# Attention output normalised transposed, one step later: reciprocal of the sums in slot 9, output and gamma rows on GpSimd's queue

## The reference

```python
def _sln(h, w, ln_g, ln_b, Wg, bg, Wb, bb):
    mu = jnp.mean(h, axis=-1, keepdims=True)
    var = jnp.mean((h - mu) ** 2, axis=-1, keepdims=True)
    ln = (h - mu) / jnp.sqrt(var + EPS) * ln_g + ln_b
    gamma = (w @ Wg.T + bg)[:, None, :]
    beta = (w @ Wb.T + bb)[:, None, :]
    return gamma * ln + beta
h = _sln(hidden, w, ln_g, ln_b, Wg, bg, Wb, bb)
qkv = (h @ Wqkv.T + bqkv).reshape(B, N, num_heads, hd, 3)
# q, k, v: the last axis, heads moved ahead of the tokens
energy = jnp.einsum('bhqd,bhkd->bhqk', q, k)
att = jax.nn.softmax(energy, axis=-1) / D ** 0.5
out = jnp.einsum('bhqk,bhkd->bhqd', att, v)
out = jnp.moveaxis(out, 1, 2).reshape(B, N, D)
out = out @ Wp.T + bp
h1 = out + hidden
h2 = _sln(h1, w, ln_g, ln_b, Wg, bg, Wb, bb)
return h2 + h1
```

## Time and profile before

| what | value |
|---|---|
| median of 3 runs | 347.56 us (345.03 to 347.65) |
| the profiled execution's own time | 345.56 us |
| its span | 343.8 us |
| PE busy | 332.5 us, 97% |
| PE's weight loads busy | 286.8 us, 83% |
| DVE busy | 298.3 us, 87% |
| ACT busy | 242.8 us, 71% |
| POOL busy | 159.1 us, 46% |
| DMA | 48.87 MB, 142 GB/s over the span |
| granted clock of PE | 1.0 of full speed |

### The profile page before, as it was taken

How to read it: one execution, slowest core, us unless ns; L and a number is a source line. 1 busy time by engine, 2 the same in 40 slices (tenths; PEclk the granted TensorE clock), 3 DMA queues, 4 the chain that set the end, 5 groups by cost and what they waited for, 6 DMA issues and landing times.

```text
span 343.8 us, 8981 instructions
## 1 busy us (share of the span) xinstructions
PE 332.5 (97%) x3173; PEld 286.8 (83%) x3173; DVE 298.3 (87%) x728; ACT 242.8 (71%) x476; POOL 159.1 (46%) x187
## 2 busy tenths in 40 slices
PE   8888999999999999999999999999999999999993
PEld 4677879888888988888888988888898988888773
DVE  4888978799898989899898989989898988999684
ACT  7664876868676786868686876868687786766740
POOL 5765544437164545527264644617254643224330
PEclk9999999999999999999999999999999999999999
DMA  7396445456555454555545454655556354652021
GB/s 242 126 218 186 124 115 140 129 155 157 170 141 156 134 152 135 173 156 170 142 125 169 134 155 134 184 142 160 161 135 157 98 157 123 182 146 67 16 61 61
DMA packets 47705, 48.87 MB, mean 142 GB/s; under 512 B 6287, under 2 KB 41374, under 8 KB 47662
## 3 DMA queue, kind: packets, MB, share of 16 engines
q1 hardware_dynamic: 44494, 46.74, 49.2%
q10 hardware_dynamic: 1184, 1.07, 1.2%
q0 software_dynamic: 1984, 0.51, 0.8%
HBM read 9.99 MB, written 4.23 MB: 41 GB/s over the span
## 4 chain that ended last, share of the span: by engine, by line
PE 87%; DVE 5%; DMA 3%; ACT 1%; issue 1%; ACTq 1%; SPq 0%; DVEq 0%
PE m L976 24%; PE st L976 19%; PE sa L976 18%; PE pv L976 17%; PE pv L1065 4%; DVE mx L692 3%; PE pv L1146 2%; PE m L1105 2%; DMA wqkv<-WqkvT_dram 2%; DMA kst<-qk_l 1%; PE pv L1079 1%; PE m L1079 1%; ACT p L602 0%; DVE qk_l L727 0%; ACTq L625 0%
## 5 line engine op out<-in xcount | busy, mean ns | idle before, releaser
L692 DVE TENSOR_REDUCE mx<-sa 128x2 f32<-128x512 f32 x256 | 171.5, 684 | 28.4 <-PE sa L976 27.3
L602 ACT ACTIVATE p<-st 128x512 f32<-128x512 f32 x240 | 140.9, 598 | 37.5 <-PE st L976 33.2
L976 PE MATMUL sa<-kst,qst 126*128 126x256 f32 x512 | 105.6, 288 | 2.0 <-DMA kst<-qk_l 1.0
L976 PE MATMUL st<-qst,kst 128*128 128x256 f32 x496 | 104.1, 292 | 0.2
L976 PEld LDWEIGHTS st<-qst,kst 128*128 128x128 f32 x496 | 75.1, 188 | 13.8 <-issue 12.8
L976 PEld LDWEIGHTS sa<-kst,qst 126*128 126x128 f32 x512 | 78.6, 189 | 4.6 <-DVE mx L692 1.7
L368 POOL DMA_DIRECT2D qst<-m_h x31 | 17.6, 567 | 112.4 <-DVE m_l L701 112.4
L976 PE MATMUL pv<-p,v_st 128*32 128x256 f32 x1008 | 61.0, 382 | 0.0
L976 PEld LDWEIGHTS pv<-p,v_st 128*32 128x32 f32 x1008 | 29.5, 109 | 21.0 <-ACT p L602 1.5
L976 PE MATMUL m<-hT_h,wqkv_h 128*128 128x256 f32 x128 | 36.8, 300 | 1.3 <-ACT hT_h L616 0.7
L377 POOL TENSOR_SCALAR xn<-xa,mv,rstd 128x256 f32<-128x256 f32 x28 | 34.2, 1227 | 1.5
(11 more groups left out here) (149 smaller groups left out, 566.2 us busy)
## 6 DMA issues: line engine op xcount, KB each, us to landing
qst<-qk_h SPq DMA_DIRECT2D x64, 128.0 KB, 2.4
qst<-qk_l SPq DMA_DIRECT2D x64, 128.0 KB, 2.5
kst<-qk_h SPq DMA_DIRECT2D x62, 128.0 KB, 2.5
kst<-qk_l SPq DMA_DIRECT2D x62, 128.0 KB, 2.8
xa<-x_dram SPq DMA_DIRECT2D x16, 256.0 KB, 3.0
gb<-gb_rows SPq DMA_DIRECT2D x16, 256.0 KB, 3.9
out_dram<-y SPq DMA_DIRECT2D x15, 256.0 KB, 3.4
wqkv<-WqkvT_dram SPq DMA_DIRECT2D x1, 512.0 KB, 5.6
```

The source lines that it names most:

```text
L602: nc.scalar.activation(p32[:, h, :], st_ps[h % 2][:], ACT.Exp).then_inc(exp_done, 1)
L692: dve.tensor_reduce(mx[:, par(a), h // HH, (h % HH) * TT:(h % HH + 1) * TT], sa_ps[h % 2][:].rearrange("p (t n) -> p t n", t=TT), AX.X, AL ...
L976: return nc.tensor.matmul(o, l, r, start=start, stop=stop)
```

## The change

For the items 0 to 13 (`by_transfer`) the output is no longer turned by token. The columns of `v_st` are interleaved (v, constant, v, constant), and `by_rows` reorders the rows of the projection's weights and the bias of v to match. SP moves the 64 channel rows of a group from `oT` into `o_rows` (the memory of `wqkv`, which is free by then) and one row of sums for each head into `sums`, 128 x 32 (`send_out`). DVE takes one reciprocal in slot 9, two transfers gather it into `recs` (the memory of `wb`), one spreads it over 128 partitions into `o_rec` (the memory of `wg`), and DVE multiplies once, 128x512, in slot 3 of the next step. ACT makes the high part from it in slot 4, POOL the low part. The projection and the residual stages of an item come one step later. `norm1` of item b + 4 moves to slots 11 to 13, with a power of its own on POOL in slot 15. The output and the rows of gamma and beta are issued by POOL, in slot 13 (`send_y`, `send_gb`). Group 0 is evicted in slot 14. The products of the projection run with the low part of `att` last. Items 14 and 15 are still turned by token (`normalise_tokens`). The last step projects items 13, 14 and 15.

```diff
-S_MT1, S_AT, S_MT0, S_XT = 1, 10, 9, 10
+S_MT1, S_AH, S_MT0, S_XT = 1, 4, 9, 10
...
-NX = 6
-S_O1, S_O0 = 3, 12
-S_OT1, S_OT0 = 6, 14
+NX = 7
+S_O1, S_O0 = 3, 14
+OUT_PRODUCTS = [(l, r, k, t) for l, r in ((0, 0), (0, 1), (1, 0)) for k in range(2) for t in range(2)]
...
-        att = sb("att", [P, TT, D])
+        sums = sb("sums", [P, H * N // P])
+        recs = wb[0:2 * HH].rearrange("p k n -> p (k n)")
+        o_rows = [wqkv[:, :, D:2 * D], wqkv[:, :, 2 * D:3 * D]]
+        o_rec, att = wg, wqkv[:, :, 0:D]
...
+        def by_transfer(a):
+
+            return 0 <= a < B - 2
...
+            def send_out(a, g):
+
+                if not by_transfer(a):
+                    return
+                half_rows = slice(g * P // 2, (g + 1) * P // 2)
+                sp.wait_ge(oT_ready, 2 * a + g + 1)
+                wait(sp, recs_in, 32 * a)
+                sp.dma_start(sums[half_rows, :], oT[1:P:32, g, :]).then_inc(sums_in[g], 16)
+                wait(sp, aTh_ready, a - 1)
+                wait(sp, aTl_ready, a - 1)
+                sp.dma_start(o_rows[par(a)][half_rows], oT[0:P:2, g, :].rearrange("p (c n) -> p c n", c=2)).then_inc(o_in[g], 16)
+
+            def gather_rec(a):
+
+                if not by_transfer(a):
+                    return
+                sp.wait_ge(rec_ready, a + 1)
+                for n in range(2):
+                    sp.dma_start(recs[n:2 * HH:2, :], sums[:]).then_inc(recs_in, 16)
+
+            def spread_rec(a):
+
+                if not by_transfer(a):
+                    return
+                sp.wait_ge(recs_in, 32 * (a + 1))
+                wait(sp, rows_ready, a)
+                sp.dma_start(o_rec[:], recs.rearrange("r (d n) -> r d n", d=1)
+                             .broadcast_to([2 * HH, HD // 2, 2 * N])).then_inc(rec_in, 16)
...
+                    if g == 0 and t == 0:
+                        gather_rec(a - 3)
...
+                send_out(b - 1, 1)
                 if has(b + 4) and has(b):
                     wait(sp, xn_ready, 1 * (b + 2) + 1)
-                    wait(sp, h1_ready, 1 * (b - 2) + 1)
+                    wait(sp, h1_ready, 1 * (b - 3) + 1)
                     sp.dma_start(xbuf(b + 4), x_t[b + 4]).then_inc(x_in[(b + 4) % 4], 16)
...
+                if not has(b + 2):
+                    gather_rec(b - 1)
+                spread_rec(b - 1)
...
-                if has(b - 1):
-                    wait(sp, y_ready, 1 * (b - 3) + 1)
-                    if first(b - 1):
-                        sp.wait_ge(gb_out, 16)
-                    sp.dma_start(gb[:, par(b - 1)], gb_dram[b - 1].rearrange("(a n) -> a n", a=1)
-                                 .broadcast_to([P, 2 * D])).then_inc(gb_in[par(b - 1)], 16)
-                if has(b - 2):
-                    wait(sp, y_ready, 1 * (b - 2) + 1)
-                    sp.dma_start(out_t[b - 2], y[:, par(b - 2)]).then_inc(y_out[par(b - 2)], 16)
+                send_out(b, 0)
...
+            def send_gb(a):
+
+                if first(a):
+                    pool.wait_ge(gb_out, 16)
+                wait(pool, y_ready, 1 * (a - 2) + 1)
+                pool.dma_start(gb[:, par(a)], gb_dram[a].rearrange("(a n) -> a n", a=1)
+                             .broadcast_to([P, 2 * D])).then_inc(gb_in[par(a)], 16)
+
+            def send_y(a):
+
+                wait(pool, y_ready, 1 * a + 1)
+                pool.dma_start(out_t[a], y[:, par(a)]).then_inc(y_out[par(a)], 16)
...
+            def low_att(a):
+
+                wait(pool, aTh_ready, a + 1)
+                pool.tensor_tensor(aT_l[:], o_rows[par(a)], aT_h[:], ALU.subtract).then_inc(aTl_ready, 1)
...
+                    if h == 0 and has(b - 1):
+                        add_bias(b - 1)
+                    if h == 1 and has(b) and has(b + 3):
+                        norm_x(b + 3)
+                    if h == 4 and by_transfer(b - 2):
+                        low_att(b - 2)
+                    if h == 5 and has(b - 3):
+                        rstd_out(b - 3)
...
-                    if h == 6 and has(b - 2):
-                        add_beta(b - 2)
-                    if h == 5 and has(b + 3) and has(b):
-                        norm_x(b + 3)
-                    if h == 0 and has(b - 1):
-                        add_bias(b - 1)
+                    if h == 6 and has(b - 3):
+                        add_beta(b - 3)
+                    if h == 15 and has(b + 4):
+                        rstd_x(b + 4)
                     if h in (13, 14) and b == B - 2:
                         add_bias(b + h - 13)
                     if h == 12:
                         low_h(b + 3)
+                    if h == 13 and has(b - 3):
+                        send_y(b - 3)
+                    if h == 13 and has(b - 2):
+                        send_gb(b - 2)
 
...
+                wait(act, o_in[g], 16 * a)
                 nc.scalar.activation(oT[:, g, :], pv_ps[g][:], ACT.Copy).then_inc(oT_ready, 1)
+
+            def high_att(a):
+
+                wait(act, rows_ready, 1 * a + 1)
+                wait(act, proj_done, 1 * (a - 1) + 1)
+                nc.scalar.activation(aT_h[:], o_rows[par(a)], ACT.Copy).then_inc(aTh_ready, 1)
...
-                    if h == S_AT + 1 and has(b - 1):
-                        wait(act, attT_done, 1 * (b - 1) + 1)
-                        wait(act, proj_done, 1 * (b - 2) + 1)
-                        nc.scalar.activation(aT_h[:].rearrange("p k n -> p (k n)"), pv_ps[1][:],
-                                             ACT.Copy).then_inc(aTh_ready, 1)
+                    if h == S_AH and has(b - 2):
+                        high_att(b - 2)
...
+            def reciprocal(a):
+
+                if not by_transfer(a):
+                    return
+                for g in range(2):
+                    wait(dve, sums_in[g], 16 * (a + 1))
+                dve.reciprocal(sums[:], sums[:]).then_inc(rec_ready, 1)
+
+            def normalise(a):
+
+                if not by_transfer(a):
+                    return
+                for g in range(2):
+                    wait(dve, o_in[g], 16 * (a + 1))
+                wait(dve, rec_in, 16 * (a + 1))
+                dve.tensor_tensor(o_rows[par(a)], o_rows[par(a)], o_rec[:], ALU.mult).then_inc(rows_ready, 1)
+
+            def normalise_tokens(a, g):
...
-                    (3, 0): [lambda: residual(b - 2, 0), lambda: residual(b - 2, 1)],
-                    (4, 0): [lambda: residual(b - 2, 2), lambda: norm1(b + 3, 0)],
-                    (4, 1): [lambda: residual(b - 2, 3), lambda: norm1(b + 3, 1)],
-                    (5, 0): [lambda: norm1(b + 3, 2)],
+                    (3, 0): [lambda: residual(b - 3, 0), lambda: residual(b - 3, 1), lambda: normalise(b - 2)],
+                    (4, 0): [lambda: residual(b - 3, 2)],
+                    (4, 1): [lambda: residual(b - 3, 3)],
                     (5, 1): [lambda: low_qk(b + 2, 0, m0, qh_ready, ql_ready)],
-                    (7, 0): [lambda: normalise(b - 1, 1, 0)],
+                    (9, 0): [lambda: reciprocal(b - 1)],
                     (7, 1): [lambda: low_qk(b + 2, 1, m1, kh_ready, kl_ready)],
-                    (8, 0): [lambda: normalise(b - 1, 1, 1)],
-                    (9, 1): [lambda: residual(b - 2, 4)],
-                    (11, 0): [lambda: low_max(b + 1, 0), lambda: low_att(b - 1), lambda: residual(b - 2, 5)],
-                    (15, 0): [lambda: normalise(b, 0, 0)],
-                    (15, 1): [lambda: normalise(b, 0, 1)],
+                    (9, 1): [lambda: residual(b - 3, 4)],
+                    (12, 1): [lambda: norm1(b + 4, 1)],
+                    (13, 1): [lambda: norm1(b + 4, 2)],
+                    (10, 1): [lambda: low_max(b + 1, 0), lambda: residual(b - 3, 5)],
+                    (11, 0): [lambda: norm1(b + 4, 0)],
                 }
+                if b == B - 2:
+                    between[(15, 0)] = [lambda: normalise_tokens(b, 0)]
                 if first(b):
                     between[(1, 1)] = between.pop((2, 1))
                 if first(b + 1):
...
+            residual(B - 4, 0)
+            low_max(B - 1, 1)
+            normalise(B - 3)
+            for stage in (1, 2, 3):
+                residual(B - 4, stage)
+            last_out(B - 2, 1)
+            residual(B - 4, 4)
+            normalise_tokens(B - 2, 1)
+            residual(B - 4, 5)
             residual(B - 3, 0)
-            low_max(B - 1, 1)
...
+            def project_out(a, quarter):
+
+                for n in range(3 * quarter, 3 * quarter + 3):
+                    l, r, k, t = OUT_PRODUCTS[n]
+                    if n == 0:
+                        wait(pe, aTh_ready, a + 1)
+                    if n == 8:
+                        wait(pe, aTl_ready, a + 1)
+                    o = mm(m1[:, t * D:(t + 1) * D], (aT_h, aT_l)[l][:, k, t * P:(t + 1) * P], (wp_h, wp_l)[r][:, k, :],
+                           n == 0, n == 11)
                 if quarter == 3:
...
```

(18 more changed lines are left out.)

160 lines of the change are left out of this document (78 added, 82 removed).

## The result

The changed kernel takes 350.78 us (median; 346.82 to 359.69), the kernel before 345.12 us (345.00 to 347.65), beside each other on one chip. The ratio is 1.0121 with a 95% interval of 1.0095 to 1.0147. The forecast of 330.5 us, range 326 to 342, was wrong by 20 us and in sign. The profiled execution took 350.8 us, its span is 348.9 (before 345.6 and 343.8). Medians are taken over all executions of a kernel, ratios and intervals only over those within 1.5% of its fastest one.

The account below looks back on a forecast made before the run. PE, busy for all 19.50 us of a middle step, was taken as the bound. 345.6 - 18.5 (transposes) + 1.3 (small waits) + 1.2 (last step) = 329.6 us; forecast as a median 330.5, range 326 to 342.

Parts of the forecast that it names:

- The price of the transposes: On PE, three groups of 0.44 us leave per item: 1.32 us a step, 18.5 us over 14 items.
- POOL's sends: Two added 128-row transfers issued by POOL in a step, expected at 0.5 to 1.1 us each, costing PE nothing.
- T: POOL's time for both sends in a step: 1 to 2 us taken, bounds 1.04 and 8.3, harmless under 2.2.
- The product on DVE: New 128x512 product in slot 3, priced at 0.748 us; a rival had `norm_x` holding it, 338 us, chance 0.08.
- Reserve 0.7 to 1.4 us: nothing is lost: SP's group 0 of the next stack, two gathers in between: data land before `scores_max` of head 0 needs them.
- SP's queue is late: Rival: slower landing or a gather's wait makes group 0 up to 0.7 us late, 13 steps, 339 us; chance 0.12.
- some 2 us of reserve: SP's group 1 of the stack starts about 1 us later, behind `send_out` of group 0, covered until slot 8.
- DMA engines are still a third idle: Argument against SP's queue is late: added bytes raise the DMA share only from 0.54 to 0.69.
- The last steps: Last step: added residual work on DVE and POOL costs 1.2 us, with bounds 0 to 4.7.
- Idle time is nearly twice the work: Last step: DVE's 8.8 us idle against 0 to 4.7 us added, the reason for taking 1.2 near the low end.

Follow-up runs that it names:

- kernel 3: The changed kernel with the spread of the reciprocals cut to 16 of 128 partitions (32 KB for 256, output wrong): nine of its 12 steps take 18.2 us.
- kernel 18: The kernel with the tiny transfers, its spread cut to 16 of 128 partitions (output wrong): 34.3 us less by the medians, 12 steps in 219.4 us.
- the kernel with the tiny transfers: Kernel 11 plus three four-byte transfers in SP's queue where gathers and spread stood: 376.93 us.
- 11: The changed kernel with the two gathers and the spread issued by ACT on its own queue, slots 10 and 13: 342.59 us, ratio 0.9873.
- 13: Kernel 11 with gamma rows and output issued by SP again, behind k: 338.57 us, ratio 0.9786.
- 15: The changed kernel with the spread alone issued by ACT (slot 14), the gathers staying on SP: 358.78 us.
- 16: The changed kernel with gamma rows and output issued by SP again, gathers and spread staying on SP: 354.33 us.
- 4: The kernel before with all transfers of the change added, results unused, POOL sending gamma rows and output: 350.79 us, ratio 1.0166.
- 10: The changed kernel with the last two sends (gamma rows of item 15, output of item 14) on SP: median hardly moved, executions 343.37 to 353.58 us.
- 5: The kernel before with output and gamma rows issued by POOL in slot 13 and not by SP, nothing else: 348.54 us.
- kernel 2: The changed kernel with gathers and spread issued by POOL (slots 10 and 13) in place of SP: 346.67 us.
- 17: The kernel with the tiny transfers, POOL's middle-item output and gamma rows cut to 8 of 128 partitions (output wrong): 14.6 us less by the medians.

## Why the prediction was wrong

**What held.** The price of the transposes: 18.2 us for a step, in nine steps of kernel 3, and 14.0 of 14.6 us in kernel 18. POOL's sends: 0.56 and 0.59 us each, T = 1.15, inside the 1 to 2 taken. The product on DVE: 675 ns for 748, and not held by `norm_x`. From the groups by shape of the changed kernel:

```profile
L789 DVE TENSOR_TENSOR wqkv<-wqkv,wg 128x512 f32<-128x512 f32 x14 | 9.5, 675 | 0.2 <-DMA wg<-wb 0.2
L441 POOL DMA_DIRECT2D gb<-gb_rows x16 | 9.0, 560 | 0.0
L447 POOL DMA_DIRECT2D out_dram<-y x15 | 8.9, 591 | 5.1 <-DVE y L905 5.1
```

**The step that failed is SP's** ("Reserve 0.7 to 1.4 us: nothing is lost"). It was made of medians and undisturbed pairs: issues of 0.6 to 0.68 us, a landing of 2.8. Its slot and its mechanism were named right, and the rival "SP's queue is late" had 0.12 with a price of 9 us. The stall above, beside the forecast: from SP's first transfer of group 0 the tenth should start after 5.4 to 6.1 us, land after up to 8.9 and be needed after 9.6; it started after 6.9 (247.02 to 253.94; the first pair alone took 2.23), landed after 11.1 and was needed after 8.9. The late start of the tenth is 0.8, the landing 1.4, the earlier need 0.7, less 0.7 of reserve: 2.2 us, the stall. The pair of 1.88 us in the kernel before stands in the very group that was priced at 5.5 us. Three numbers were wrong. The landing that counts is that of the transfer PE waits for, 4.16 in the stall above with a median of 2.7 on the page: in that stall the output, the gamma rows and the spread are in flight just then, because POOL sends in slot 13 what SP had sent behind k. The issue of the rows soon after the spread costs up to 2.5 us instead of 0.63; group 1, to which I gave "some 2 us of reserve", begins behind it, and waits of 0.5 to 1.4 us in slot 8 follow. And "DMA engines are still a third idle" weighed bytes: the spread was counted as 256 KB like any other, by the 3.9 us of the gamma rows. It lands after 4.6 us at best, and per byte it takes nearly three times the engines' time.

**What is shown of the cause:** cutting the spread's size gives back 5.7 of the 8.2 us missing in the 12 steps where it stands in SP's queue (3), and in the kernel with the tiny transfers all that they had cost (18); taking gathers and spread out of SP's queue gives back 4.9 and 5.4 with all bytes in place (11, 13), but the spread alone out of it makes things worse (15); more time for issues on SP makes PE wait though k lands fast (16); the same transfers under steps of 19.5 us cost the steps nothing (4). So both the queue and the spread's engine time take part, and they become visible only once PE's step is shorter. What draws an issue out is not shown: the kernel before and 3 and 18, with their small spreads, have pairs of 1.9 to 2.2 us too, at other places. A stall also costs more than its length: in kernel 3 two stalls of 2.2 and 2.8 us lengthened their steps by 3.9 and 3.6 (22.1 against 18.2, and 21.3 against 17.7 for the same step in 18), the clock being at its lower level for part of what follows (in the second PE waits for `mx` as well).

**The last steps** had 1.2 us, with bounds 0 to 4.7. Without the kst stalls (18) the last three steps cost 51.4 - 49.1 = 2.3, and the tail without its stall (10, 13) 16.0 - 14.4 = 1.6: 3.9 us, within the bounds and three times the value taken. "Idle time is nearly twice the work" was no reason: the work is a chain of small steps between DVE and POOL, and PE waits for its end. The changed kernel's own tail has another 2.8 for `xn` and the low clock, in the profiled execution; in eight variants it has not, and their end is 1.9 longer instead. Tail and end together lost 5.5 us in it and 4.9 to 5.0 in those.

**The end** was no term at all. In every kernel in which POOL sends the rows (5 has nothing else), apart from kernel 2, the execution ends some 2.5 us later after POOL's last instruction; in the changed kernel 1.1 of it shows as "end", since the slow last products on PE come after that instruction, and the rest is hidden in the tail.

In sum for the profiled executions: 12 steps -6.4 in place of -14.6, the rest up to the tail's end +0.5 + 5.6 + 4.4, the end +1.1.

## What to carry to other kernels

When the bounding engine's list gets shorter, the transfers behind it lose the same time: price the cover of each by the slowest landing in company with what will be in flight then, not by the page's median. Two transfers of one size are not one price; read a queue's share of the engines' time beside its bytes. Transfers with slack went behind those that the bounding engine waits for, in the same queue, and the chain of small transfers with its slow end went to another engine's queue: kernel 13, which does both, is 3.3% faster than the changed kernel (ratios 0.9786 and 1.0121) and 2.1% faster than the one before (interval 1.7 to 2.6). The first alone (16) is slower than the changed kernel.

## What the runs showed of the hardware

- A broadcast of 16 partitions' rows to 128 (256 KB, SBUF to SBUF) landed after 4.6 to 6.5 us in the changed kernel, a transfer of x of the same size after 3.2 (median). Whether this comes from the 16 source partitions or from the writes was not tried; the Trainium skill (DMA: Bandwidth & Descriptors, section "The descriptor swizzle") lists the writes of a transfer to 128 partitions in groups of four neighbours to a port; if reads went by the same list, 16 neighbouring rows would be read through 4 of 16 ports, an estimate that no run here shows.
- The issue of group 0's rows on SP, soon after the spread, took 0.64 to 2.5 us in the changed kernel, up to 3.2 with the spread in ACT's queue (15) and 2.1 with it in POOL's (2); with a spread of 32 KB never more than 0.66 (3, 18).
- The execution ended 6.05 to 6.16 us after the start of POOL's last instruction in the four kernels where POOL sends only the maxima (and y(14)), 8.4 to 8.7 us in fifteen where it sends rows, 4.05 us in kernel 2, where it sends most. The bytes of the middle items' rows do not matter (17: 8.60). The cause stays open.
